# Eight fused layers on one core: two projection banks in turn in the local layers, weights issued inside the first stage, and a normalization moved forward

## The reference

```python
x = x + _L0_attn_ref(_layernorm(x), Wq, Wk, Wv, Wo, W_feat)     # "favor": linear attention, 16 heads of 64
x = x + _L0_ffn_ref(_layernorm(x), ...)                         # "router"
x = x + _L1_attn_ref(_layernorm(x), ...)                        # "cosine" attention
x = x + _L1_ffn_ref(_layernorm(x), ...)                         # "int4" linear layer
x = x + _L2_attn_ref(_layernorm(x), ...)                        # "mamba": state space scan, 256 channels x 16 states
x = x + _L2_ffn_ref(_layernorm(x), ...)                         # "experts"
x = x + _L3_attn_ref(_layernorm(x), ...)                        # "hgrn": gated recurrence
x = x + _L3_ffn_ref(_layernorm(x), Wqkv, q_scale, k_scale, Wo, ln_g, ln_b, W1, b1, W2, b2)   # "local"
```

```python
q = l2norm(q) * qs;  k = l2norm(k) * ksc                        # attention layer, heads of 64
q = q * cos * scale + rotate_half(q) * sin * scale
k = k * cos / scale + rotate_half(k) * sin / scale
out = softmax(8 * q k^T, masked to the band) v                   # windows of 32
x = shift(x) ... + out @ Wo
xn = (x - mu) / sqrt(var + 1e-5) * g + b                         # MLP layer
a, gate = split(xn @ W1 + b1);  x = x + (a * gelu(gate)) @ W2 + b2
```

## Time and profile before

| | |
|---|---|
| median of three runs | 6522.08 us |
| the profiled execution | 6522.74 us, of which the span of the trace is 6520.8 us |
| TensorE busy over the span | 5878.9 us (90%) |
| VectorE, ScalarE, GpSimd busy | 4384.8 (67%), 3402.6 (52%), 2289.2 (35%) |
| first matmul of the favor stage | 41.41 us from the span's start |
| first projection of the local layers | 3236.59 us, last at 6425.8 us |

### The profile page before, as it was taken

The page is one execution under the profiler, slowest core; times in us unless marked ns, Lnnn a source line. Parts: engine busy times, 40 slices in busy tenths (PEclk is TensorE's granted clock), DMA queues, the critical chain, the costliest instruction groups (busy, mean ns, idle before and its releaser), DMA issues.

```text
span 6520.8 us, 129965 instructions
## 1 busy us (share of the span) xinstructions
PE 5878.9 (90%) x51681; PEld 3219.8 (49%) x51681; DVE 4384.8 (67%) x7178; ACT 3402.6 (52%) x5560; POOL 2289.2 (35%) x1597
## 2 busy tenths in 40 slices
PE   7999878999677778998689999999999999999998
PEld 3555554444422225765445555555555555555554
DVE  4656434454288894334678888888878788887885
ACT  3444324656144443444456656666666666665664
POOL 0111101222034441000055555555555555555553
PEclk9999978999688888998799999999999999999998
DMA  5555302333100000000011111111111111111110
GB/s 138 115 115 119 89 0 53 80 82 83 44 3 0 0 0 1 1 0 1 24 36 32 40 43 34 31 47 37 34 45 38 33 44 40 34 39 41 38 37 24
DMA packets 298945, 275.95 MB, mean 42 GB/s; under 512 B 40580, under 2 KB 289572, under 8 KB 298148
## 3 DMA queue, kind: packets, MB, share of 16 engines
q1 hardware_dynamic: 298372, 268.00, 17.7%
HBM read 30.88 MB, written 2.10 MB: 5 GB/s over the span
## 4 chain that ended last, share of the span: by engine, by line
PE 33%; issue 5%; DVE 5%; POOL 5%; ACT 2%; DMA 0%; POOLq 0%; DVEq 0%; SPq 0%; ACTq 0%
PE banks L2254 7%; PE banks L2289 6%; PE banks L2324 5%; PE banks L2309 4%; PE banks L2267 3%; PE banks L2341 3%; DVE local_probs L2559 2%; POOL local_rot L2653 2%; POOL local_ssum L2645 2%; PE banks L2363 2%; PE banks L2313 2%; PE banks L2274 1%; ACT local_probs L2455 1%; DVE local_gate L2584 1%; DVE local_sin L2540 1%
## 5 line engine op out<-in xcount | busy, mean ns | idle before, releaser
L2645 POOL TENSOR_TENSOR local_ssum<-local_sq 128x512 f32<-128x512 f32 x384 | 697.5, 1816 | 2145.1 <-ACT local_sq L2433 2144.6
L2653 POOL TENSOR_TENSOR local_rot<-local_rot,local_inv_all 128x512 f32<-128x512 f32 x768 | 964.6, 1288 | 94.1 <-DMA local_inv_all<-local_inv 93.6
L2254 PE MATMUL banks<-local_y,local_Wqkv 128*128 128x512 f32 x1536 | 823.0, 618 | 64.0 <-ACT local_sq L2433 61.2
L2559 DVE TENSOR_TENSOR local_probs<-banks,band 128x576 f32<-128x576 f32 x768 | 546.2, 753 | 185.4 <-PE banks L2289 180.1
L2455 ACT ACTIVATE local_probs<-local_probs,local_npeak 128x1152 f32<-128x1152 f32 x384 | 482.8, 1257 | 357.1 <-DVE local_probs L2559 357.1
L2539 DVE TENSOR_TENSOR local_rot<-banks,local_rotary_scaled 128x512 f32<-128x512 f32 x768 | 525.6, 684 | 191.1 <-PE banks L2254 185.6
L2433 ACT ACTIVATE local_sq<-banks 128x512 f32<-128x512 f32 x768 | 459.4, 598 | 253.6 <-DVE local_sin L2540 244.8
L2546 DVE TENSOR_TENSOR local_rot<-local_rot,local_sin 128x1024 f32<-128x1024 f32 x384 | 513.7, 1338 | 41.9 <-DVE local_sin L2540 2.3
L2449 ACT COPY local_v<-banks 128x512 f32<-128x512 f32 x384 | 224.9, 586 | 594.1 <-PE banks L2267 593.6
L2289 PEld LDWEIGHTS banks<-local_rot 32*128 32x128 f32 x12288 | 416.7, 186 | 225.0 <-issue 200.8
L2540 DVE TENSOR_TENSOR local_sin<-banks,local_rotary_scaled 128x512 f32<-128x512 f32 x768 | 522.4, 680 | 0.0
(11 more groups left out here) (400 smaller groups left out, 10561.4 us busy)
## 6 DMA issues: line engine op xcount, KB each, us to landing
local_inv_all<-local_inv SPq DMA_DIRECT2D x768, 128.0 KB, 2.7
favor_half_norm_all<-favor_half_norm SPq DMA_DIRECT2D x512, 128.0 KB, 3.0
cosine_inv_all<-cosine_inv SPq DMA_DIRECT2D x256, 128.0 KB, 2.6
favor_rden<-favor_inv SPq DMA_DIRECT2D x256, 64.0 KB, 2.1
cosine_rden<-cosine_inv_den SPq DMA_DIRECT2D x256, 64.0 KB, 2.1
local_Wqkv<-in_L_ffn_Wqkv_quads SPq DMA_DIRECT2D x36, 256.0 KB, 2.9
local_Wo<-in_L_ffn_Wo_quads SPq DMA_DIRECT2D x6, 512.0 KB, 4.1
experts_w_W<-in_L_ffn_W SPq DMA_DIRECT2D x1, 2048.0 KB
```

Source lines behind the costliest of these rows:

```text
L2254: pe.matmul(seqs(banks[:, QK_BANK, :]), Wqkv[:, at:at + P], y_group(g), start=True, stop=True).then_inc(qk_projected, 1)
L2559: dve.tensor_tensor(probs[:, e % 3, r:r + 2, :], banks[:, S_BANK + r:S_BANK + r + 2, 0:SCORES], consts["band"].unsqueeze(1).broadcast_to([ ...
L2645: pool.tensor_tensor(ssum[:, n % 2, m, :], sq[:, 0, :], sq[:, 1, :], ALU.add).then_inc(square_summed, 1)
L2653: pool.tensor_tensor(a, a, twice(inv_all[:, n % 2, m, of_seq(s)]), ALU.mult).then_inc(united, 1)
```

## The change: what it does

There are three parts.

1. **Start.** SP's first block issues four constants instead of nine, favor's weights and x, and no more. The other five constants are issued by SP inside favor's loop at step 1, and the weights of router, cosine, int4, mamba and hgrn at steps 2 to 6, each behind that step's `send_norm`.
2. **State space stage.** `MEASURE`, `NORMALIZE`, `TURN`, `TURNED` move to places -4 to -1, that is four to five steps ahead; `project_out` is cut into two halves at places 3 and 4, and `ADD_OUT` moves to 5.
3. **Local layers.** The block ahead of the loop treats only group 0; the layer norm and transposes of groups 1 to 7 run inside steps 0 to 7. Projections go to banks 0 and 1 in turn (`qk_bank`): even ones to bank 0, which they share with the denominators, odd ones to bank 1, which they share with v. So `project(4i+1)` and `project(4i+3)` wait for `copy_v`, `project_v` waits for `square` of the odd projection before it, and the even ones wait for the logarithm of the denominators. `score` stands ahead of `project_v`, `norm` behind it. The denominators are computed before the values. ScalarE squares before it copies v, and takes the logarithm of the denominators ahead of `exp`, their exponential behind the next `square`. The rotary tables of a layer are scaled in two halves, the first one a step earlier.

```diff
@@ build
-                for n in consts:
+                for n in FAVOR_CONSTS:          # ident, ones, heads_of_pair, causal
                     sp.dma_start(consts[n], t[n]).then_inc(consts_loaded, 16)
                 ws["favor"].load(sp)
                 sp.dma_start(x[:, GT:TILES, :], rows[:, GT:TILES, :]).then_inc(x_rest, 16)
-                for name in ("router", "cosine", "int4", "mamba", "hgrn"):
-                    ws[name].load(sp)
...
@@ favor_attention, SP's loop over i
                     if (n := within(i - 1)) is not None:
                         send_norm(n)
+                    if i == LOADS:
+                        for tile, source in w["later_consts"]:
+                            sp.dma_start(tile, source).then_inc(w["consts_loaded"][0], 16)
+                    if 0 < i - LOADS <= len(w["later"]):
+                        w["later"][i - LOADS - 1].load(sp)
+                sp.wait_ge(*w["consts_loaded"])
@@ state_space
     MEASURE, NORMALIZE, TURN, TURNED, WIDEN, LOWER, BIAS, LOWER_C, BIAS_C, LAST_DT, SPLIT_ALL, SOFTPLUS, DELTA = \
-        0, 1, 2, 3, 5, 7, 8, 9, 10, 11, 12, 13, 14
-    GATE, WAY_OUT, ADD_OUT = 2, 3, 4
-    FIRST, LAST = -NS, N + ADD_OUT
+        -4, -3, -2, -1, 5, 7, 8, 9, 10, 11, 12, 13, 14
+    GATE, WAY_OUT, ADD_OUT = 2, (3, 4), 5
+    FIRST, LAST = MEASURE - NS, N + ADD_OUT
...
-                def project_out(g):
+                def project_out(g, half):
                     pe.wait_ge(gated, CH * (g + 1))
-                    for t in range(GT):
+                    for t in range(half * GT // 2, (half + 1) * GT // 2):
...
@@ local_layers
+    qk_bank = lambda c: (DEN_BANK, V_BANK)[c % 2]
...
-                for tile in range(TILES):
-                    dve.bn_stats(ln_stats[:, tile, :], x[:, tile, :]).then_inc(stats_done, 1)
...
+                measure(dve, 0)
...
-                for g in range(GROUPS):
-                    pe.wait_ge(normed, (g + 1) * GT)
...
+                turn_x(pe, 0)
...
@@ TensorE, project(c)
-                    if c:
-                        pe.wait_ge(squared, c)
+                    if half:
+                        pe.wait_ge(v_copied, c // 2 + 1)
+                    elif n >= 3:
+                        pe.wait_ge(den_logged, 2 * n - 5 + m)
+                    elif c:
+                        pe.wait_ge(squared, c - 1)
...
@@ TensorE, project_v(j)
-                    if j >= 6:
-                        pe.wait_ge(den_logged, j - 5)
-                    elif j:
-                        pe.wait_ge(v_copied, j)
+                    if j:
+                        pe.wait_ge(squared, 2 * j)
...
@@ TensorE, values(e): the denominators first, in DEN_BANK
+                    if at_step < N:
+                        pe.wait_ge(squared, 4 * at_step + 3 - 2 * s)
...
+                    last.then_inc(den_summed, 1)
                     pe.wait_ge(v_copied, min(e + 6, 2 * N))
...
@@ TensorE, the loop over i
                         project(4 * i)
+                    if (e := within(2 * (i - 2))) is not None:
+                        score(e)
+                    if i < N:
                         project_v(2 * i)
                     if 1 <= i <= N:
                         norm(i - 1)
-                    if (e := within(2 * (i - 2))) is not None:
-                        score(e)
...
+                    if 1 <= i < GROUPS:
+                        take_x(y_ready, 2 * (i + 1))
+                        turn_x(pe, i)
@@ ScalarE, the loop over i
                     if i < N:
+                        square(4 * i)
                         copy_v(2 * i)
-                        square(4 * i)
                     if 1 <= i <= N:
                         invert_norm(i - 1)
+                    if (e := within(2 * (i - 3) + 1)) is not None:
+                        log_den(e)
                     if (e := within(2 * (i - 2))) is not None:
                         exp(e)
                     if i < N:
                         square(4 * i + 1)
                     if (e := within(2 * (i - 3) + 1)) is not None:
-                        take_den(e)
+                        invert_den(e)
...
-                    if (e := within(2 * (i - 2) + 1)) is not None:
-                        exp(e)
+                    if 1 <= i < GROUPS:
+                        copy_x(act, i)
                     if (G := mlp_at(i, 8)) is not None:
                         square_mlp(G)
                     if (G := mlp_at(i, 9)) is not None:
                         take_gate(G, 0)
+                    if (e := within(2 * (i - 2))) is not None:
+                        log_den(e)
+                    if (e := within(2 * (i - 2) + 1)) is not None:
+                        exp(e)
...
@@ VectorE, the loop over i
-                            scale_tables(i // STEPS)
-                        rotate_start(4 * i)
+                            scale_tables(i // STEPS, 1)
+                    if (e := within(2 * (i - 2))) is not None:
+                        mask(e)
                     if 1 <= i <= N:
                         clamp(i - 1)
-                    if (e := within(2 * (i - 2))) is not None:
-                        mask(e)
...
+                    if i < GROUPS - 1:
+                        measure(dve, i + 1)
...
+                    if i < GROUPS - 1:
+                        normalize_x(dve, i + 1)
```

More of the change, by code:

```diff
@@ L1274, in _ @@
                         gather(k - 2)
-                    if (g := finish_at(k, WAY_OUT)) is not None:
-                        project_out(g)
+                    for half in range(2):
+                        if (g := finish_at(k, WAY_OUT[half])) is not None:
+                            project_out(g, half)
                     if (m := make_at(k, TURN)) is not None:
@@ L2534, in rotate_start @@
                     k = 2 * n + m
+                    if n % STEPS == 0 and half == 0:
+                        dve.wait_ge(tabled, 8 * layer_of(n) + 4 * m + 4)
                     dve.wait_ge(qk_projected, c + 1)
@@ L2722, in _ @@
                 sp.wait_ge(stored, 16 * GROUPS)
+FAVOR_CONSTS = ("ident", "ones", "heads_of_pair", "causal")
 STAGES = ["favor", "router", "cosine", "int4", "mamba", "experts", "hgrn", "local"]
@@ L2860, in _ @@
                 sp.dma_start(x[:, GT:TILES, :], rows[:, GT:TILES, :]).then_inc(x_rest, 16)
-                for name in ("router", "cosine", "int4", "mamba", "hgrn"):
-                    ws[name].load(sp)
-                sp.wait_ge(consts_loaded, 16 * len(consts))
-                if stages[0] != "favor":
+                sp.wait_ge(consts_loaded, 16 * len(FAVOR_CONSTS))
+        later_consts = [n for n in consts if n not in FAVOR_CONSTS]
+        ws["favor"].tiles["x_loaded"] = (x_first, x_rest)
+        ws["favor"].tiles["later"] = [ws[name] for name in ("router", "cosine", "int4", "mamba", "hgrn")]
+        ws["favor"].tiles["later_consts"] = [(consts[n], t[n]) for n in later_consts]
+        ws["favor"].tiles["consts_loaded"] = (consts_loaded, 16 * len(consts))
+        if stages[0] != "favor":
+            with nc.Block() as block:
+                @block.sync
+                def _(sp):
+                    for n in later_consts:
+                        sp.dma_start(consts[n], t[n]).then_inc(consts_loaded, 16)
+                    for name in ("router", "cosine", "int4", "mamba", "hgrn"):
+                        ws[name].load(sp)
+                    sp.wait_ge(consts_loaded, 16 * len(consts))
                     sp.wait_ge(x_first, 16)
                     sp.wait_ge(x_rest, 16)
-        ws["favor"].tiles["x_loaded"] = (x_first, x_rest)
         for stage in stages:
```

139 lines of the change are left out of this document (82 added, 57 removed).

## The result

The change made the kernel slower, by little: 6534.3 us against 6520.5 us for the kernel before on the same chip, 20 runs of each, ratio 1.0020 with a 95% interval of 1.0013 to 1.0026. The forecast was 6505 us and faster. The time lies inside the range of 6450 to 6570; the direction is wrong. The profiled execution has a span of 6538.8 us (6520.8 before); it was the slowest of the 20 of after, 6.5 us above their median, so differences between the two traces come out a few us larger than those of the medians.

A forecast was written before the change was run, and what follows sets the result against it. TensorE was taken to bound the local layers, half of the span, and VectorE the state space stage. Terms -18 - 8 - 15 + 24 = -17 took 6522 to 6505 us; range 6450 to 6570.

The forecast's parts named there:

- Start, -18: Start and favor: 23 us won by an earlier first take of a projection, 5 given back to moved loads.
- State space, -8: State space stage: 3.5 us from transposes, 3.5 from first-group preparation leaving the scan, 1 from halves that fit.
- Ahead of the loop, -15: Before the local loop: it starts 22 us earlier, less 7 us for preparation moved into its first eight steps.
- The local steps, +24: Local layers: 118 us of new waits and distances against 94 us of old waits gone; bounds -23 and +90.
- The walk: Local step timed from profile distances: first to second projection goes from 3.58 to 3.77 us.
- The isolated norm, 36 us: Local steps, TensorE: norm no longer leans on the scores, 0.19 us in each of 192 steps.
- The least wait for the copy, 35 us: Local steps: `project(4i+1)` waits at least 0.18 us for `copy_v` in each of 192 steps.
- The waits for `hide`, 15 us: One local step in four: projection late by 0.8 instead of 0.18 us; 30 us in full, half taken.
- the second rival: Local layers lose more than the rest wins: copy of v closes a ring through VectorE every step; 6581 us, chance 0.25.
- `add_out`, 7 us: Local step behind the output projection: `add_out` on VectorE adds 0.15 us to the projection's lateness.
- The wait of v in the quiet step, 25 us: Local step without MLP matmul in its first half: v waits 0.52 us for `square(4i+1)`, in 48 groups.
- Gone: the 94 us: Local layers: all TensorE waits before, 61.2 us for `square`, 19.7 and 13.1 us ahead of the norm, disappear.

The follow-up runs named there:

- the third run: Kernel before plus new start, new state space stage and preparation spread over the first local steps; local order and banks as before: 6479.0 us, ratio 0.9943.
- the short `hide`: Kernel after with VectorE's product of gate and widened values done for 64 of 512 columns: 6508.8 us, ratio 0.9986.

## Why the prediction was wrong

*Start, -18.* Right: -19.4 at the first statistics of cosine. Both of its parts were larger than forecast and nearly cancel: 25.4 gained (23 forecast, since x landed at 18.70 and not at 21), some 6 given back (5). *State space, -8.* Right: -10.2, and the wait at 43.6 us as forecast (40 to 45). *Ahead of the loop, -15:* -21.6 at its first projection, and the preparation put into it cost 9 (7 forecast). Together -41 forecast, -42 measured by those differences, and the third run is 38 below before.

*The local steps, +24, failed:* +72 less the preparation's 9 is +63, and this is where the sign turned. The term that was mis-sized is the wait of `project(4i+1)` for the copy of v. The walk gave it 35 + 15 + 7 = 57 us; measured are 84 us in 183 steps, some 88 in 192. The 31 us between are as much as the whole forecast was off (-17, measured +14). (The upper bound of +90 is not what the terms give in full: 70 + 35 + 30 + 7 + 25 - 94 is +73.) Term by term:

- The isolated norm, 36 us: right in size. The kernel with the new order and the old banks lost 31 us, with the distance of the walk (3.78 against 3.77).
- The least wait for the copy, 35 us: right as a least, 0.17 to 0.18 us in the quiet step.
- The waits for `hide`, 15 us: this is the step of the working that failed. The text had the copy behind `square(4i)` and that behind VectorE, found 0.8 instead of 0.18 in one step of four, "in full 30 us", and took half. It is 0.89 on average in that kind of step: 0.71 more in 48 groups, 34 us. The reason for the half was that TensorE had waited for the same `hide` 29 times before; but those waits, 19.7 us, were already in the 94 that were taken off, so they were counted twice. The run with the short `hide` bears the cause out: 0.46 us less of it gave 0.35 back. The "just in time" of the other steps held in the quiet kind (0.19) and not in the third, which has 0.17 more than the walk (8 us); steps 5 and 6 add 5. The term of the copy in all is 0.46 us a step, past the 0.27 that the second rival named as deciding and near its 0.5, but without its ring in every step.
- `add_out`, 7 us: right (0.31 against 0.33).
- The wait of v in the quiet step, 25 us: 16, of which 11 are new. In after the distance from `project(4i+2)` to v is 1.19 us there (4571.40 to 4572.63 in one of them, with the square of the odd projection as releaser); it was 0.96 before, and is 0.86 in the other kinds.
- "Gone: the 94 us": 78. Of the norm's 32.8 us, 14.5 stayed, and 1.2 of the squares' 61.2.

With these, +24 + 19 + 8 + 5 - 5 - 14 + 16 = +53, where +63 was measured; the 10 us that are left stay open. The mechanism was seen, and the second rival described it; its size was cut by a guess that engines recover between steps. Both orders in which norm and scores touch have the same least from first to second projection, 3.56 us, and the order in which they don't costs 31 us. The Trainium skill, page "TensorEngine Tiling (Array Packing)", section "Key Properties", says that a change of tiling mode drains TensorE; the trace agrees, with 0.17 us more in the median (3.78 against 3.61) for one change more. That a drain is what takes this time is not shown.

The experiments cut the same +63 us of loop (3198.6 with old steps, 3261.4 after) in another way, each piece the difference of two runs: the new order on the three engines with the old banks +31 (3229.9); the two banks, the early logarithm, ones ahead of values, tables in halves and the copy first, all together, -21 (3209.1); and, in that kernel, the copy behind the square +52. The middle piece was not taken apart, and the swap of copy and square was not tried with the old banks. The walk noted that the copy stands behind the square and called its 35 us the least; it never asked what a copy ahead of the square would give. How the +52 arises is seen in the rows of single steps; that a square is late for GpSimd in the third kind of step was not tried by itself.

## What to carry to other kernels

When a new order puts an instruction of another engine on the path of the busiest one, look at what stands ahead of it in its own queue: here a copy whose data were ready waited behind a square whose data were not, and swapping the two was worth 52 us of loop, more than the order of the stages on the busiest engine (31 us). A lateness found in a walk through a steady loop is paid in every round; take it in full (here 30 us, 34 measured, 15 forecast) unless a row shows the round in which it is recovered, and take care that a wait that was there before is credited once. A change of many parts is best timed part by part: here three parts won 38 us and the fourth lost 52 (38 + 13.8).

## What the runs showed that I had not expected

- The early logarithm and the shared banks go together. In the kernel with v, norm, scores the norm waits 61 us with the early logarithm and 24 us with the late one, but with the late one projections wait 57 us for the bank. That the early one does it by holding back the last square was not tried by itself.
- A rotation's last operation on VectorE, the addition over 128x1024, took 1.23 us in most cases and up to 2.32 in others, the same shape. In after the 70 of 384 that took over 1.5 us had GpSimd working during 95% of their time, the 285 under 1.3 us during 5%. In before it is less clear: there GpSimd worked during 53% of the short ones as well. Whether these two engines hold each other up was not tried.
